# A graph network kernel on one core: softmax layers 2 and 3 split gathered rows on the chip instead of reading a table of split rows

## What is computed

```
def _softmax_aggregate(msg, dst, n):
    m = jax.ops.segment_max(msg, dst, num_segments=n)
    ex = jnp.exp(msg - m[dst])
    denom = jax.ops.segment_sum(ex, dst, num_segments=n)
    alpha = ex / denom[dst]
    return jax.ops.segment_sum(msg * alpha, dst, num_segments=n)

def _genconv(x, src, dst, W1, b1, g, be, W2, b2):
    msg = jax.nn.relu(x[src]) + EPS_MSG
    out = _softmax_aggregate(msg, dst, n) + x
    h = out @ W1 + b1
    ...                      # batch norm over the nodes, relu
    return h @ W2 + b2
```

## Time and profile before

| quantity | value |
| --- | --- |
| median of 3 runs | 3636.91 us (3635.1 to 3639.06) |
| span of the profiled execution | 3635.8 us |
| phase of layer 1, dense work | 766.3 to 1213.4 us |
| phase of layer 2, from its first ScalarE instruction to its last | 1276.3 to 1811.9 us |
| dense work of layer 2 | 1336.15 to 1788.7 us |
| dense work of layer 3, end | 2362.3 us |

### The profile page before, as it was taken

One profiled execution on the slowest core, in us unless ns is written; L12 is line 12 of the kernel. 1 busy time (PEld: TensorE's weight loads), 2 busy tenths in 40 slices (PEclk: granted clock), 3 DMA queues, 4 the chain that ended last, 5 costly groups with the idle time before them and its releaser, 6 DMA issues. The chain is left out here.

```text
span 3635.8 us, 71136 instructions
## 1 busy us (share of the span) xinstructions
PE 3043.8 (84%) x20101; PEld 2475.3 (68%) x20101; DVE 2221.1 (61%) x5687; ACT 1926.0 (53%) x3685; POOL 2387.2 (66%) x2488
## 2 busy tenths in 40 slices
PE   2799993069999759999759999966999999999997
PEld 0466662058888648888658888865777777777775
DVE  6665551034555654555564545575888888888887
ACT  0432221046667556666556666664555555655555
POOL 1777777777766257666356767515777777777773
PEclk7799997579999869999869999988999999999998
DMA  9586552088888378878467878747556555565552
GB/s 330 181 284 213 182 182 75 0 275 283 261 256 253 97 277 275 263 245 263 151 256 240 264 252 261 231 127 203 156 161 162 160 162 160 161 161 159 159 161 77
DMA packets 421706, 728.99 MB, mean 201 GB/s; under 512 B 75617, under 2 KB 259355, under 8 KB 415618
## 3 DMA queue, kind: packets, MB, share of 16 engines
q0 software_dynamic: 132992, 330.52, 30.2%
q1 hardware_dynamic: 273863, 329.88, 29.9%
q10 hardware_dynamic: 14651, 66.23, 4.7%
HBM read 576.97 MB, written 149.39 MB: 200 GB/s over the span
## 5 line engine op out<-in xcount | busy, mean ns | idle before, releaser
L2243 POOL DMA_INDIRECT ring<-h_table,idx_ring x832 | 813.6, 978 | 272.5 <-issue 251.7
L627 POOL DMA_INDIRECT pair_rings<-split_table,src_idx x768 | 767.8, 1000 | 324.2 <-issue 216.6
L1593 PE MATMUL ps<-casts,two_parts 128*128 128x500 f32 (+1 forms) x3768 | 846.8, 380 | 24.2 <-DVE two_parts L1685 13.2
L1593 PEld LDWEIGHTS ps<-casts,two_parts 128*128 128x128 f32 x3768 | 682.8, 191 | 150.7 <-DVE two_parts L1685 14.9
L640 POOL DMA_INDIRECT adjacency<-acc x508 | 491.9, 968 | 225.0 <-issue 151.6
L1685 DVE TENSOR_TENSOR two_parts<-work,two_parts 128x512 fp32r<-128x512 f32 x300 | 204.0, 680 | 501.1 <-ACT two_parts L1480 500.9
L1492 ACT ACTIVATE casts<-spare 128x1000 fp32r<-128x1000 fp8e4 (+1 forms) x471 | 458.9, 974 | 0.0
L2340 ACT ACTIVATE work<-acc,vecs 128x512 f32<-128x512 f32 x208 | 150.2, 722 | 440.9 <-DVE acc L2401 362.1
L1626 PE MATMUL ps<-pair_rings,hot_r 128*128 128x256 f32 x1536 | 216.4, 293 | 183.4 <-DVE hot_r L523 170.2
L1480 ACT ACTIVATE two_parts<-work 128x512 fp32r<-128x512 f32 x300 | 185.8, 619 | 320.7 <-PE ps L1593 319.8
L1626 PEld LDWEIGHTS ps<-pair_rings,hot_r 128*128 128x128 f32 x1536 | 194.7, 194 | 187.0 <-DVE hot_r L1751 171.0
(11 more groups left out here) (337 smaller groups left out, 5879.1 us busy)
## 6 DMA issues: line engine op xcount, KB each, us to landing
spare<-adjacency SPq DMA_DIRECT2D x216, 250.0 KB, 4.1
acc<-e_few SPq DMA_DIRECT2D x208, 256.0 KB
work<-msg_table SPq DMA_DIRECT2D x144, 256.0 KB, 5.0
split_table<-acc ACTq DMA_DIRECT2D x32, 1024.0 KB, 4.4
work<-in_edge_attr SPq DMA_DIRECT2D x104, 256.0 KB
e_few<-spare SPq DMA_DIRECT2D x52, 512.0 KB
spare<-rel_rows SPq DMA_DIRECT2D x208, 84.0 KB
spare<-adjacency SPq DMA_DIRECT2D x72, 187.5 KB, 4.2
```

Source lines behind the costliest of these rows:

```text
L627: e.indirect_dma_start(out=to, out_offset=None, in_=table, in_offset=bass.IndirectOffsetOnAxis(ap=src_idx[:, 2 * i + h, j:j + 1], axis=0)) ...
L1593: ins = e.matmul(bank, two_parts[:, d % 2, b % 2, q, kind * D:(kind + 1) * D], cast_counts[n % CASTS][:, at:at + width], start=opens, stop ...
L2243: e.indirect_dma_start(out=rows[:, s, j, :], out_offset=None, in_=h_table, in_offset=bass.IndirectOffsetOnAxis(ap=idx_ring[:, s, j:j + 1], ...
```

## The change

In layers 2 and 3 there is no split table. All 42 pairs gather plain rows of 512 bytes from `msg_table` into the slot in which their parts will stand, and ScalarE and VectorE make the parts there, pair by pair: for each of the two halves of a pair an `exp` of 128 x 512, a multiplication of the same size, a copy of 128 x 1024 to the high part, and a subtraction of 128 x 1024 to the low part. The 13 units, their loads and stores, and the special treatment of the first 5 pairs are gone; all pairs are summed by L1626's form of two parts. The new instructions stand at the end of ScalarE's and VectorE's step `i`. TensorE's step `i` now begins with one block, then transposes, the other blocks, and last the sum of pair `i - 1`; ScalarE takes the sums of pair `i - 1` out behind the first duo of its step. SP loads rows for the dense work first. `FIRST_STEP` goes from 3 to 0 and `STEP_COLUMNS` from 4720 to 4600, for layer 1 as well; layer 1 still gathers from its split table.

```
-FIRST_STEP = 3
-STEP_COLUMNS = 4720
+FIRST_STEP = 0
+STEP_COLUMNS = 4600
...
-            whole = 0 if ready else WHOLE
+            raw = 0 if ready else PAIRS
...
+                def exp_of_pair(i, h):
+                    rows = half_values[2 * slot_of(i) + h]
+                    half_landed(e, S, i, h)
+                    e.activation(rows[:, :, 1, 0:D], rows[:, :, 0, 0:D], ACT.Exp, bias=negc[:, :]).then_inc(S("p_exp"), 1)
+
+                def high_of_pair(i, h):
+                    parts = half_slots[2 * slot_of(i) + h]
+                    e.wait_ge(S("p_mul"), 2 * i + h + 1)
+                    e.activation(parts[:, :, 0, :], half_values[2 * slot_of(i) + h][:, :, 1, :], ACT.Copy).then_inc(S("p_high"), 1)
...
-                    if d == 0:
-                        space_made(e, S)
...
-                    for d in duos_at(i):
+                    duos = duos_at(i)
+                    for d in duos[0:1]:
                         dense_duo(d)
+                    if 0 <= i - 1 < raw:
+                        nodes_of_pair(i - 1)
+                    for d in duos[1:]:
+                        dense_duo(d)
...
+                    if 0 <= i < raw:
+                        for h in range(2):
+                            exp_of_pair(i, h)
+                        for h in range(2):
+                            high_of_pair(i, h)
...
+                    blocks = [n for n in range(ALL_BLOCKS) if step_of(n) == i]
+                    first = 1 if 0 <= i - 1 < raw else 0
+                    for n in blocks[0:first]:
+                        block(n)
+                    if 0 <= i - 2 < PAIRS:
+                        turn_pair(i - 2)
...
+                    if raw <= i - 1 < PAIRS:
+                        sum_pair(i - 1)
+                    for n in blocks[first:]:
+                        block(n)
+                    if 0 <= i - 1 < raw:
+                        sum_pair(i - 1)
...
+                def times_of_pair(i, h):
+                    rows = half_values[2 * slot_of(i) + h]
+                    e.wait_ge(S("p_exp"), 2 * i + h + 1)
+                    e.scalar_tensor_tensor(out=rows[:, :, 1, D:2 * D], in0=rows[:, :, 0, 0:D], scalar=EPS_MSG, in1=rows[:, :, 1, 0:D],
+                                           op0=ALU.add, op1=ALU.mult).then_inc(S("p_mul"), 1)
+
+                def low_of_pair(i, h):
+                    parts = half_slots[2 * slot_of(i) + h]
+                    e.wait_ge(S("p_high"), 2 * i + h + 1)
+                    e.tensor_tensor(parts[:, :, 1, :], half_values[2 * slot_of(i) + h][:, :, 1, :], parts[:, :, 0, :].bitcast(F32),
+                                    ALU.subtract).then_inc(S("p_low"), 1)
...
                     for d in duos_at(i):
                         dense_duo(d)
+                    if 0 <= i < raw:
+                        for h in range(2):
+                            times_of_pair(i, h)
+                        for h in range(2):
+                            low_of_pair(i, h)
```

More of the change, by code:

```diff
@@ L99, in slot_of @@
 def slot_of(i):
-    return (i if i < WHOLE else i - WHOLE - 1) % SLOTS3
+    return i % SLOTS3
 def landed(layer, i):
@@ L516, in gnn_kernel @@
         half_slots = [pair_rings[:, k, :, :, :] for k in range(2 * SLOTS3 - 1)] + [end_rows[:, :, :, :]]
+        half_values = [pair_values[:, k, :, :, :] for k in range(2 * SLOTS3 - 1)] + [end_values[:, :, :, :]]
         def pair_onehot(e, i, columns, to_hot=None):
@@ L1400, in load_dense_rows @@
                     e.dma_start(dense_rows[j % 2][:, 0:n, :], by_block[:, u * UNIT:u * UNIT + n, :]).then_inc(S(f"dense_rows_in{j % 2}"), 16)
+                for j in range(2):
+                    load_dense_rows(j)
                 for d in range(3):
@@ L1426, in pool @@
                 for i in range(PAIRS):
-                    reached(e, S("sums"), free_after(i, whole))
+                    reached(e, S("sums"), free_after(i))
                     if ready and i == SLOTS3 - 1:
                         e.wait_ge(S("agg_out"), 16)
-                    if not ready and i == WHOLE:
-                        for b in range(5):
-                            e.wait_ge(S(f"split_out{b}"), stored_units(max(u for u in range(UNITS) if made_in(u) == b)))
-                    pair_gathers(e, S, i, whole)
+                    pair_gathers(e, S, i, raw)
@@ L1686, in dense_duo @@
                                     ALU.subtract).then_inc(S("d_low"), 1)
-                if not ready:
-                    times_rows(0)
-                    for u in range(2):
-                        unit(u)
                 e.wait_ge(S("zero"), 2 * SLOTS)
@@ L1788, in dve @@
                 e.wait_ge(S("stats"), 2 * NJOBS)
-            names = ("params kept over quot node exp mexp acc sums turned by_node zero onehot W1 hid stats "
-                     "rows_in0 rows_in1 rows_in2 rows_in3 dense_rows_in0 dense_rows_in1 v_exp v_mul v_high v_low counts_in0 counts_in1 counts_in2 dense divisor_kept product_kept "
-                     "d_exp d_mul d_high d_low cast agg_out blank "
-                     "dense_over dense_quot evacuated").split() + [f"split_out{b}" for b in range(5)]
+            names = ("params kept over quot node acc sums turned by_node zero onehot W1 hid stats p_exp p_mul p_high p_low "
+                     "dense_rows_in0 dense_rows_in1 counts_in0 counts_in1 counts_in2 dense divisor_kept product_kept "
+                     "d_exp d_mul d_high d_low cast agg_out blank dense_over dense_quot evacuated").split()
             def general_sync(e, S):
```

193 lines of the change are left out of this document (43 added, 150 removed).

## The result

| | before | changed |
|---|---|---|
| median of the runs | 3637.18 us (4 runs) | 3742.93 us (4 runs, 3742.09 to 3743.68) |
| ratio to before | 1 | 1.0294, 95% interval 1.0279 to 1.0308 |
| span of the profiled execution | 3635.8 us | 3740.3 us |
| TensorE busy | 3043.8 us (84%) | 3064.7 us (82%) |
| VectorE busy | 2221.1 us | 2469.6 us |

The change moved 148 MB less and was 2.9% slower. 3751 was predicted, with a range of 3695 to 3825.

A forecast was written before the change was run, and what follows sets the result against it. TensorE bounded the dense stretch before; after the change a ScalarE-VectorE loop would. Each raw layer gains 49 us and pays 96 + 14, two layers +122, layer 1 -7: 3635.8 + 122 - 7 = 3751 us, range 3695 to 3825.

The forecast's parts named there:

- The head start: Layers 2 and 3: dense blocks need not wait for the split table, first block near 1287, 49 us gained a layer.
- The loop: Dense stretch, raw layers: ScalarE and VectorE wait for each other, 8.3 us a step plus 2.77 per duo after the first.
- Quotients: VectorE, dense stretch of a raw layer: three regions, two chunks each, 6 x 4.9 = 29 us.
- Region changes: Dense stretch: emptying the banks stands behind a pair, 3 x 6.7 = 20 us a layer, bounds 3.65 and 10 each.
- The clock: TensorE, dense stretch: slow matmuls after long stalls, 8 us a layer of a possible 27, bounds 0 and 27.
- Rival B: TensorE's clock falls in every step of layers 2 and 3: 3890 us, chance 8%.
- Rival C: POOL's gathers, slowed beside VectorE to 1.76 us each, pace the steps: 3761 us, chance 3%.
- Rival A: TensorE stays the bound, dense stretch stays at 452 us or so: 3559 us, chance 6%.
- Its milder form: The loop exists, but quotients, statistics and region changes fall into VectorE's idle time: 3627 us, chance 5%.
- The tail: Raw layers, after the last block: three pairs summed with nothing overlapping, 38 us, 14 more than before.
- ScalarE's wait: Sign in layer 2's dense stretch: ScalarE's exp waits for VectorE's low part 80 us or more, 39.5 before.
- Layer 1: No raw pairs; first block near 753, 13 us earlier, less some costs: -7 us, bounds -15 and +8.

The follow-up runs named there:

- the doubled reciprocals: Changed kernel with every reciprocal of a region's quotients done twice in layers 2 and 3: 3794.99 us, ratio 1.0434.
- the halves: Changed kernel with only the reciprocals of the regions' quotients split into halves in successive steps: 3733.64 us, ratio 1.0267; 4291.3 us on the slower chip.

## Why the prediction was right, step by step

**The head start** was to be 49 us, first block near 1287. From the table load to the first block it was 59.9 us and is 11.1: 48.8. The block stands at 1283.17, since layer 1 had won 4.2:

```profile
1283.17 9.21 PE L1525 MATMUL ps<-casts,two_parts 128*128 128x500 f32 x32 [12.14 <-DVE two_parts L1615]
```

**The loop** of 8.3 us and 2.77 per further duo: steps with two duos 10.9 to 11.2, with three 13.8 to 14.0, in the last region 13.1 (13.71 with statistics of 0.65); predicted 11.1, 13.8 and 13.0. From the `add_up` at 1314.15 to the one at 1827.54 there are 37 steps. 37 x 8.3 + 39 x 2.77 + 17 x 2.35 + six quotients of 4.9 and 17 statistics of 0.65 are 495.5 us, and they took 513.4. (The prediction counted 14 further duos of the last region; the program has 17, and 41 in place of 44 of the others, 1 us less.)

**Quotients** stood in the loop in full: 16.24 - 10.95 - 0.65 = 4.6 us and 15.82 - 10.95 = 4.9, and doubling them shows the same from the other side.

**Region changes** were taken at 6.7 each (bounds 3.65 and 10). The steps in which they fall were 8.9, 0.6 and 6.2 us longer than their terms in the sum, together 15.6 and not 20; why the second cost so little was not looked into. The first of them on TensorE, to be held against the earlier trace rows:

```profile
1414.10 3.67 PE L1525 MATMUL ps<-last_cast,two_parts 128*128 128x500 f32 x8 [8.05 <-DVE acc L1660]
1417.57 3.09 PE L1525 MATMUL ps<-casts,two_parts 128*128 128x500 f32 x8
```

**The clock** had 8 us a layer (bounds 0 and 27), and 5 can be found. The slow matmuls are there: after the stall of 8.05 us 16 of them took 6.8 us, at about half pace, and TensorE's busy time in the stretch grew by 22.4 us where one more pair explains 2.1. Mostly TensorE fell behind in steps in which it would have waited, so the growth replaced waits. In three steps it fell so far behind that the loop waited for it. The first, behind a stall in the quotients:

```profile
1468.96 3.70 PE L1525 MATMUL ps<-casts,two_parts 128*128 128x500 f32 x8 [3.72 <-DVE two_parts L1615]
...
1472.66 6.60 PE L1525 MATMUL ps<-casts,two_parts 128*128 128x500 f32 x24
1479.10 2.07 PE L1548 MATMUL ps<-pair_rings,hot_r 128*128 128x256 f32 x16
```

```profile
1481.21 0.38 ACT L1451 ACTIVATE work<-ps 84x256 f32<-84x256 f32 x1 [2.46 <-PE ps L1548]
```

Full pace is 1.97 and 5.62 for these blocks, so the pair's sum came some 2.7 us late; ScalarE waited 2.46 us for it ahead of its next duo, and the step from 1476.62 took 15.60 us where its terms give 13.8. The steps from 1740.47 and 1759.61 are 1.2 and 2.0 us longer than their terms in the same way: ScalarE's copy waits 1.12 and 1.58 us for TensorE's blocks, which ran at a granted clock of 0.83 and 0.77 behind stalls of 5.65 and 4.75. Together 5.0 us; what the clock added inside the region changes is not taken apart.

So of the 17.9 us that 513.4 has over 495.5, region changes are 15.6 and the clock 5.0, and the other steps came out 2.8 below their terms, mostly 0.1 each. For these 37 steps the prediction was 10 us too high; for what lies ahead of the first and behind the last it was 3.6 too low (29.1 measured, 25.5 left of its 549). The 542.5 us of the stretch are therefore nearer to 549 than the terms are. Two of the named signs follow from TensorE's slow matmuls in place of waits: its busy share was 85% and not 80%, and the waits for the pair's parts were 13 us and not 40.

**Rival B** (the clock falls in every step, 3890) is refuted. At 1389.01 a block of 8 matmuls took 2.10 us behind a wait of 1.49 us, where 1.97 is full pace, and the stretch around it was granted 1.00, the level of 2.4 GHz:

```profile
1380.00:1410.00 30.00, 23.90 (x121) 19.71 (x119) 19.90 (x33) 25.22 (x38) 23.90 (x21) 1.00 0.42 120
```

Behind the stall of 8.05 us above they ran at half pace. The Trainium skill, "TensorE: Matmul & The Clock Gate", on HAM oscillation, describes a kernel whose waits are longer than the bursts of matmuls between them, and there every burst starts cold. The prediction told this without that condition. The waits of 1.5 us here are shorter than the bursts of some 9 us between them, so they are not that case; that matmuls behind a long wait start cold, the trace agrees, with the stall of 8.05 us.

**Rival C** (POOL paces the steps, 3761) falls too, though its mechanism is in the trace. Gathers of the raw rows, at a median of 0.95 us, have a mean of 1.12:

```profile
L630 POOL DMA_INDIRECT pair_values<-msg_table,src_idx x560 | 626.0, 1118 | 313.9 <-issue 150.1 <-PE ps L1548 98.9 <-PE ps L1525 57.0
```

This fits the mechanism; that VectorE lengthens them was not tried by a run. POOL waits 156 us for TensorE in these (two layers), so it is ahead. **Rival A** (TensorE stays the bound) needed a wait of its block under 20 us; it was 59.9. Its milder form, in which the quotients fall into VectorE's idle time, is ruled out by the doubled reciprocals.

**The tail** was to be 38 us and was 39.3: the last `add_up`s stand 7.8 us apart, 11.6 with a quotient of 500 columns between them, 8.9 with one of 250, and 3.7. **ScalarE's wait** for the low part, 80 or more, was 76.5.

**Layer 1** gave 4.2 us and not 7. Its first block came 11.7 us earlier, predicted 13:

```profile
754.60 8.99 PE L1525 MATMUL ps<-casts,two_parts 128*128 128x500 f32 x32 [174.76 <-DVE two_parts L1615]
```

but its dense stretch grew from 447 to 455 us, where I had allowed 6; its tail kept its 24. TensorE's waits for VectorE in it (755 to 1209.9), for the emptied banks and for `add_up` ahead of a pair's sum:

```profile
PE ps L1525 <- DVE acc L1660: 8.2, 3, 3.7
PE ps L1548 <- DVE onehot L1632: 7.8, 5, 2.7
```

Before the change they were 4.6 and 4.5. The runs with fewer columns a step and with split quotients each won some 9 us in this layer, 8 of them in this stretch (447 us in both): the first wait is 2.5 with 4380 columns, the second 0.5 with the halves. So the quotients, which stand ahead of `add_up` in VectorE's queue, cost time in layer 1 too.

In sum, a layer gained 48.8 and paid 90.1 and 15.3: +56.6, predicted +61. The span of 3740.3 us lies 10.5 under the sum of 3750.8: the two layers are 7.7 lower, the part up to layer 2 is 2.8 higher, and what follows layer 3, which the prediction took as unchanged, is 5.6 lower. So half of the miss lies where the prediction had no term, and some errors cancel: that the total came within 0.3% is in part luck. The mechanism and the large terms (head start, loop, quotients, tail) were each measured by themselves and are not.

## What to carry to other kernels

Before work is moved onto engines that the profile shows half idle, follow the queue orders around one step: two in-order engines that hand results to each other can close a loop longer than the step of the engine that bounds. The loop's length is set by what stands between two hand-overs and not by the sum of the work; here the same instructions in another order gave back 101 of 106 us. A cheap test for such a loop is a dummy instruction at the suspected place: paid in full it is in the loop; here it was paid to a fifth where TensorE set the pace.

## What the runs showed of the hardware

The kernel before took 3637 to 3638 us in all comparisons but one, and 4274 in that one, on another chip. There, in the halves alone, the durations of VectorE's and ScalarE's instructions in layer 2 are the same, and the layer takes 637.0 us (630.3 where the kernel before took 3637). The time went in other phases, 227 us ahead of layer 2 and 312 behind layer 3, where engines stood idle longer with nothing in the profile that they waited for. The granted clock was lower as well, 0.887 over the span for 0.929, and TensorE was busy for 3320.7 us in place of 3064.5. The first row is of that chip, in the groups of its longest waits:

```profile
L2222 PEld LDWEIGHTS ps<-mats,work 128*128 128x128 f32 x1664 | 241.7, 206 | 161.8 <-issue 160.5 <-ACT work L2287 1.2
```

and the same code (some lines higher) in the changed kernel on a chip of 3637:

```profile
L2213 PEld LDWEIGHTS ps<-mats,work 128*128 128x128 f32 x1664 | 217.9, 191 | 100.7 <-issue 99.6 <-ACT work L2278 1.1
```

What causes it, and whether the lower clock is a cause of the idle time or follows from it, was not tried. So a kernel's time is to be held against the kernel before on the same chip.
